# Four-layer attention and feed-forward kernel: a schedule table for the two threads of its middle layers

## The reference

```python
# layer 1, feed-forward: gated low-rank experts on a base product
base = jnp.einsum('bsd,od->bso', x, W_base) + b_base
gate = jax.nn.softmax(xf @ W_gate.T, axis=-1)
thr = jax.nn.sigmoid(xf @ W_thr + b_thr[0]) * MAX_THRESHOLD
adapted = gate - thr[:, None]
...
h = jnp.einsum('nd,erd->ner', xf, A_w)
moe = jnp.einsum('ner,ne,eor->no', h, w, B_w) * SCALING
# layer 2, attention: group-wise products with the context, a group norm over y
t = jnp.einsum('oc,bcd->bod', Wt, inp_v)
p = jnp.einsum('oc,bcd->bod', Wp, inp_q)
g = jnp.einsum('oc,bcd->bod', Wg, inp_k)
...
return yn * gn_w[None, :, None] + gn_b[None, :, None] + residual
# layer 2, feed-forward: 16 heads of 32 features on permuted columns
t = jnp.einsum('bhd,hdm->bhm', t, up)
t = jax.nn.gelu(t, approximate=False)
t = jnp.einsum('bhm,hmd->bhd', t, down)
```

## Time and profile before

| | us |
|---|---|
| median of 3 runs | 1979.35 |
| lowest and highest | 1978.04, 1983.15 |
| the profiled execution | 1980.43 |
| its span, from first to last instruction | 1978.6 |
| busy in the span: PE | 1773.6 |
| busy: DVE | 1457.3 |
| busy: POOL | 1094.7 |
| busy: ACT | 1066.9 |

### The profile page before, as it was taken

One profiled execution on the slowest core, in us unless ns is written; L12 is line 12 of the kernel. 1 busy time (PEld: TensorE's weight loads), 2 busy tenths in 40 slices (PEclk: granted clock), 3 DMA queues, 4 the chain that ended last, 5 costly groups with the idle time before them and its releaser, 6 DMA issues.

```text
span 1978.6 us, 26146 instructions
## 1 busy us (share of the span) xinstructions
PE 1773.6 (90%) x8645; PEld 1452.4 (73%) x8645; DVE 1457.3 (74%) x2518; ACT 1066.9 (54%) x2555; POOL 1094.7 (55%) x970
## 2 busy tenths in 40 slices
PE   6877899999999999887777699999999999879989
PEld 4655778878887888675455578888888888768777
DVE  6974798998999975676453588888888888848730
ACT  5335677777787775521334254655555545536520
POOL 7666575565565654533533366766767768526600
PEclk8878999999999999897776899999999999989999
DMA  3011211112111210200002111111111111011111
GB/s 128 1 59 40 57 57 48 49 49 69 55 43 49 70 49 23 80 25 0 0 0 80 43 38 34 38 53 38 38 38 54 33 38 38 24 49 61 44 52 38
DMA packets 54134, 88.06 MB, mean 45 GB/s; under 512 B 9008, under 2 KB 15792, under 8 KB 53744
## 3 DMA queue, kind: packets, MB, share of 16 engines
q1 hardware_dynamic: 54000, 86.39, 14.1%
HBM read 75.62 MB, written 10.75 MB: 44 GB/s over the span
## 4 chain that ended last, share of the span: by engine, by line
DVE 23%; PE 19%; issue 18%; POOLq 13%; POOL 12%; ACT 8%; DVEq 6%; DMA 0%; SPq 0%; ACTq 0%
POOLq L284 7%; DVE b_st_u L211 7%; PE e_ps L66 6%; POOLq L282 5%; DVEq L212 4%; PE c_ps L66 3%; POOL d_roped L1093 3%; PE b_ps_o L66 2%; PE b_ps_job L66 2%; POOL d_pt_sign L281 2%; ACT b_st_sign L192 2%; PE a_ps L66 2%; POOL d_wo L1098 1%; DVEq L136 1%; POOL d_wq L1098 1%
## 5 line engine op out<-in xcount | busy, mean ns | idle before, releaser
L66 PE MATMUL b_ps_o<-b_wo,b_oT 128*128 128x512 f32 x768 | 190.2, 397 | 20.4 <-DVE b_oT L1340 20.4
L66 PE MATMUL d_ps_o<-d_wo,d_oT 128*128 128x512 f32 x768 | 193.3, 401 | 12.2 <-DVE d_oT L1339 12.2
L281 POOL TENSOR_SCALAR b_pt_sign<-b_pt_sign 128x512 f32<-128x512 f32 x112 | 81.3, 726 | 206.9 <-ACT b_pt_sign L273 196.8
L66 PE MATMUL d_ps_job<-xnT,d_wq 128*128 128x512 f32 x768 | 193.3, 404 | 2.3 <-DVE d_rot_b L1349 2.3
L66 PE MATMUL b_ps_job<-xnT,b_wq 128*128 128x512 f32 x768 | 190.2, 401 | 4.8 <-DVE b_qT L1340 4.7
L66 PEld LDWEIGHTS b_ps_o<-b_wo,b_oT 128*128 128x128 f32 x768 | 145.4, 191 | 56.3 <-DVE b_oT L1340 26.2
L1093 POOL TENSOR_TENSOR d_roped<-d_rot_a,d_rot_b 128x512 f32<-128x512 f32 x80 | 104.7, 1309 | 144.1 <-DVE d_rot_b L1349 144.1
L211 DVE SCALAR_TENSOR_TENSOR b_st_u<-b_st_sign,b_st_u 128x512 f32<-128x512 bf16 x182 | 176.5, 970 | 9.5 <-issue 0.9
L66 PEld LDWEIGHTS d_ps_o<-d_wo,d_oT 128*128 128x128 f32 x768 | 144.8, 191 | 51.8 <-DVE d_oT L1339 18.9
L66 PEld LDWEIGHTS b_ps_job<-xnT,b_wq 128*128 128x128 f32 x768 | 143.1, 191 | 35.8 <-issue 6.7
L66 PEld LDWEIGHTS d_ps_job<-xnT,d_wq 128*128 128x128 f32 x768 | 143.1, 191 | 33.8 <-issue 3.5
(11 more groups left out here) (359 smaller groups left out, 4344.1 us busy)
## 6 DMA issues: line engine op xcount, KB each, us to landing
b_raw<-in_wq_dram SPq DMA_DIRECT2D x32, 256.0 KB, 2.6
b_raw<-in_wo_dram SPq DMA_DIRECT2D x32, 256.0 KB, 2.7
d_raw<-in_wq_dram SPq DMA_DIRECT2D x32, 256.0 KB, 2.6
d_raw<-in_wo_dram SPq DMA_DIRECT2D x32, 256.0 KB, 2.7
e_nat<-dequantized SPq DMA_DIRECT2D x30, 256.0 KB, 3.1
b_st_v<-in_quantized_dram SPq DMA_DIRECT2D x13, 256.0 KB, 2.9
dequantized<-b_st_u SPq DMA_DIRECT2D x13, 256.0 KB, 2.8
a_ctx_in<-in_ctx_dram SPq DMA_DIRECT2D x8, 256.0 KB, 5.3
```

Source lines behind the costliest of these rows:

```text
L66: i = pe.matmul(out, a, b, start=first and t == 0, stop=last and t == len(terms) - 1)
L281: pool.tensor_scalar(sign, sign, 0.5 * NF4_RISES[k], 0.0 if k else 0.5 * sum(NF4_RISES[:14]) - 1.0, ALU.mult, ALU.add)
```

## The change

It replaces stage c's `START` by a table in the form of stage a's: a due time for every step of each thread and engine. The steps are cut up so that each can be placed alone: the base products become steps of their own (`base`), ahead of or between those of the gates, with the four results of `low` packed in two banks to leave the others free. Norm statistics are taken tile by tile. In the up phase the gelu writes back into its PSUM bank, the high part is copied from the bank, and the low part is made by DVE instead of POOL, since it now reads PSUM; `up` h + 3 waits for that DVE step where it waited for the gelu. `tables` moves on DVE from 36 to 20.44, ahead of `z` of thread 0. SBUF is laid out anew so that stage d's first buffers are free earlier: its weight DMAs are due at D_AT - 119, its context DMAs at D_AT - 55.5, its splits' low parts go from DVE to POOL, and its first products are placed ahead of thread 1's `t4`. D_AT moves to C_AT + 224.5.

```diff
-        SPLITS = [("w", 0), ("ctx", 0), ("w", 1), ("w", 2), ("ctx", 1), ("ctx", 2), ("ctx", 3), ("w", 3), ("w", 4), ("w", 5)]
-        FIRST = [n for kind, n in SPLITS if kind == "w"]
+        FIRST = [n for kind, n, _ in SPLITS if kind == "w"]
 
         def split_at(kind, n):
-            return READ + PITCH * SPLITS.index((kind, n))
...
             def weights():
-                yield READ - 10.0
+                yield T + LOADS[0]
                 ready(sp, 0)
-                for kind, n in SPLITS[0:7]:
-                    if kind == "w":
-                        load(n)
-                    else:
-                        sp.dma_start(ctx_raw[:, n], ctxT_dram[:, n]).then_inc(s_ctx[n], 16)
+                for n in range(RAW):
+                    load(n)
                 for n in range(RAW, PER * n_groups):
                     yield low_at(n - RAW) + 0.05
                     load(n)
 
+            def contexts():
+                yield T + LOADS[1]
+                ready(sp, 1)
+                for n in range(K_CH):
+                    sp.dma_start(ctx_raw[:, n], ctxT_dram[:, n]).then_inc(s_ctx[n], 16)
+
...
-                ready(sp, 1)
+                yield T + LOADS[2]
+                ready(sp, 2)
...
-    LATER = 38.0
-    START = {"cs": (-18, 0.7), "g": (-13, 1.5), "rates": (-6, 0), "t1": (5, 2.2), "low": (13.5, 1.4), "gates": (20, 0), "hT": (30.5, 0),
-             "ffn": (33, 3.6), "norm2": (48, 0), "xs": (53, 1.3), "p": (57, 0.9), "grp": (61, 0), "y2": (64, 0.8), "x2": (64.2, 0.8),
-             "norm3": (68, 0), "t3": (73, 1.0), "pick": (77, 2.0), "up": (86, 1.5), "down": (96.5, 6.0), "out": (118, 2.0),
-             "norm4": (127, 0), "t4": (132, 1.0)}
-    PREPARED = {"wg": -18.5, "wm": -18, "wp": -17.5, "thr": -7, "wl": -4, "wb": 2, "wB": 14, "down": 28.5, "up": 35, "tables": 36}
     EARLY, RAW, OVER = -37.5, -14.5, 13.0
...
+    TIMES = {
...
+        ("pe", "low"): (13.5, 18.48, 21.12, 23.76, 40.61, 45.59, 49.73, 52.31),
...
+        ("pe", "t3"): (95.83, 96.66, 97.8, 98.8, 115.92, 117.49, 118.32, 120.14),
...
+        ("pe", "down"): (121.14, 133.8, 153.42, 164.52, 145.62, 161.22, 172.91, 188.22),
+        ("pe", "out"): (169.79, 176.21, 179.33, 182.45, 193.84, 196.72, 199.11, 201.5),
...
+        ("act", "gelu"): (110.83, 113.95, 115.41, 116.27, 118.14, 120.59, 127.73, 130.85, 139.63, 144.55, 145.93, 150.28, 152.26, 154.24, 158.77, 160.66,
...
+        ("act", "acts"): (111.69, 114.81, 117.54, 119.41, 124.61, 125.8, 128.59, 131.71, 141.01, 146.62, 147.39, 151.66, 156.89, 160.06, 161.35, 162.64,
...
+        ("dve", "z"): (26.07, 54.16),
...
+        ("dve", "thr"): (-7,), ("dve", "tables"): (20.44,)}
...
+        low_bank = lambda t: banks(t)[:, 0:2].rearrange("p b n -> p (b n)").rearrange("p (j n) -> p j n", n=LOW_PITCH)
+        base_bank = lambda t, j: bank(t, (2, 3, 1, 0)[j])
...
-                for h in H:
-                    yield at(t, "up", h + 1)
-                    waits(pool, t, ("act", "acts", h))
-                    done(pool.tensor_tensor(acts[t][:, 1, h % 4], act_f[t][:, h % 4], acts[t][:, 0, h % 4], ALU.subtract), ("acts", h))
...
+            def base(t):
+                for j in J:
+                    yield at("pe", "base", t, j)
+                    prepared(pe, "w_wb")
+                    waits(pe, t, ("dve", "t1", j), (("dve", "t1", 2), ("dve", "t1", 3), ("dve", "hw", 0), ("dve", "hT", 0))[j])
+                    product(pe, base_bank(t, j), [[xT(t, a, j)[:, c] for a in (0, 1)] for c in range(K_CH)],
                             [hi_lo(wb, c) for c in range(K_CH)], last=False)
...
                     c, r = divmod(h, 4)
                     rows = slice(32 * r, 32 * r + 32)
-                    waits(pe, t, ("dve", "pick", c if h >= 3 else h))
-                    if h >= 3:
-                        waits(pe, t, ("act", "gelu", h - 3))
-                    done(product(pe, bank(t, h % 3), [[up[rows, a, c] for a in (0, 1)]], [[xp[t][rows, a, c] for a in (0, 1)]]), ("up", h))
...
+                    yield at("pe", "up", t, h)
+                    prepared(pe, "w_up")
+                    waits(pe, t, ("dve", "pick", c), ("dve", "acts", h - 3) if h >= 3 else ("dve", "pick", h))
+                    pe_s[t].done(product(pe, bank(t, h % 3), [[up[rows, a, c] for a in (0, 1)]], [[xp[t][rows, a, c] for a in (0, 1)]]), ("up", h))
...
+            def gelus(t):
+                for h in H:
+                    yield at("act", "gelu", t, h)
                     waits(act, t, ("pe", "up", h))
-                    if h >= 4:
-                        waits(act, t, ("pool", "acts", h - 4))
-                    done(act.activation(act_f[t][:, h % 4], bank(t, h % 3), ACT.Gelu), ("gelu", h))
...
+            def highs(t):
+                for h in H:
...
                     if h >= 4:
                         waits(act, t, ("pe", "down", h // 4 - 1))
-                    done(act.copy(acts[t][:, 0, h % 4], act_f[t][:, h % 4]), ("acts", h))
...
+                    act_s[t].done(act.copy(acts[t][:, 0, h % 4], bank(t, h % 3)), ("acts", h))
...
+            def act_lows(t):
+                for h in H:
+                    yield at("dve", "acts", t, h)
+                    waits(dve, t, ("act", "acts", h))
+                    dve_s[t].done(dve.tensor_tensor(acts[t][:, 1, h % 4], bank(t, h % 3), acts[t][:, 0, h % 4], ALU.subtract), ("acts", h))
...
         def ready(eng, n):
 
 
-            waits(eng, 1, ("pe", "out" if n == 2 else "y2", 3))
-            waits(eng, int(n == 3), ("dve", "t4", 3))
+
+            if n == 0:
+                waits_all(eng, 1, ("pe", "y2"))
+                waits_all(eng, 0, ("dve", "p"), ("pool", "xc"))
+            if n == 1:
+                waits_all(eng, 0, ("pe", "down"))
+                waits_all(eng, 1, ("pool", "xb"))
+            if n in (2, 3):
+                waits_all(eng, 0, ("dve", "t4"))
+            if n == 3:
+                waits_all(eng, 1, ("pe", "out"))
+            if n == 4:
+                waits_all(eng, 1, ("dve", "t4"))
 
...
-    D_AT = C_AT + 193.0
+    D_AT = C_AT + 224.5
...
+    D_LOADS = (-119.0, -55.5, -25.0)
+    D_SPLITS = [("w", 0, -108.0), ("w", 1, -106.0), ("w", 2, -104.0), ("w", 3, -100.0), ("w", 4, -98.0),
+                ("ctx", 0, -42.0), ("ctx", 1, -39.0), ("ctx", 2, -36.0), ("ctx", 3, -33.0), ("w", 5, -24.5)]
...
-        d, d_over = grouped_attention(nc, stack, D_AT, D_AT - 50.0, 2.7, "vector", "d_", resid, xnT, w["ctxT"], w["gqa3"], w["tables3"], codes, None, (21, 8), c_ready, (-20.0, -18.0, -10.0, -5.0))
+        d, d_over = grouped_attention(nc, stack, D_AT, D_LOADS, D_SPLITS, "gpsimd", "d_", resid, xnT, w["ctxT"], w["gqa3"], w["tables3"], codes, None, (21, 8), c_ready, FIRST_UNITS)
```

621 lines of the change are left out of this document (318 added, 303 removed), and 46 rows, old and new, of the table TIMES.

## The result

The changed kernel takes 1917.91 us, the median of four runs (1915.94 to 1919.5), beside 1978.69 for the kernel before on the same chip: a ratio of 0.9692, with a 95% interval of 0.9669 to 0.9714. The profiled execution took 1918.22 us with a span of 1916.4, 62.2 less than before. In a later set of runs the same kernel took 1919.54 (ratio 0.9707, 0.9694 to 0.9721).

What follows compares the result with a forecast made beforehand. Stage c was taken as bound by waits in a circle, at a low clock. Stage c's 35.6 us and stage d's start's 6.2 us made 41.8 us: 1979.35 - 41.8 = 1937.6, say 1938 us, range 1920 to 1965.

Steps and rivals of the forecast that it cites:

- The factor: Stage c: trace time over table time, taken from stage a as 1.072, so 203.5 us for the table's 189.9.
- the factor is nearly 1 or below it: Rival, stage c: table steps may be longer than the engines'; at 1.00 time 1924, at 0.93 1911; chance 0.18.
- The clock: PE in stage c: with fewer gaps the granted clock was expected above 0.77; no size given.
- the low bound of 0.93 for the factor: Stage c: PE's estimated work of about 176 us, at a clock of 0.77, over the table's 189.9.
- `tables` costs nothing: DVE, stage c: moved ahead of `z`, the block takes 3.9 us after its DMAs land at 860.0, nothing beyond the factor.
- The bank and the gelu: Up phase: gelu in its bank taken as 0.607 us, DVE's subtraction as 0.691, bank held 1.9 us a turn.
- the other end: Up phase: gelu written to its bank takes 0.760 us by row L1832, adding 0.8 us a thread.
- the 20 that would have spoken against the forecast: Up phase: prediction wrong if PE's idle time put down to DVE's subtractions is more than some 20 us in sum.
- Stage d's start: From stage c's last `out` to stage d's first scores: 30.8 us against 37.0, 6.2 us saved.
- The splits on POOL: Stage d: splits take 2.6 us each on POOL; thread 0's root for `t4` could lose up to 2.6, taken as 0.
- threads hold each other up: Rival, stage c: in-order engines let a late step stop the other thread; factor 1.12 to 1.26, 1946 to 1973; chance 0.24.
- The signs: Profile after: `t3` of thread 1 some 110 us behind first `low`; wrong if first scores come after 1105 or before 1070.

Runs made afterwards that it cites:

- The three doubled steps: Changed kernel with one up-phase step made twice, a run each: subtraction on DVE 1931.17 us, copy on ACT 1930.67 us, `up` product on PE 1926.22 us.

## Why the prediction was wrong, point by point

**The factor is the step that failed.** I took the whole of stage a, 170.2 us for 158.8 in its table, as a rate of 1.072 and laid it on the 189.9 us of stage c: 203.5. Measured were 184.6, a factor of 0.972. That is 18.9 us, and the whole miss is 19.0. The factor was the wrong size, for two reasons. First, stage a's lag is no rate. PE in the kernel before, at the first product due at 47.2 (`we`) and the last `out` of stage a, due at 146.4:

```profile
52.10 2.93 PE L66 MATMUL a_ps<-a_wT,a_dft 128*128 128x512 f32 x6 [1.57 <-DVE a_wT L828]
...
152.58 1.63 PE L66 MATMUL a_ps<-a_wprod,a_dft 128*128 128x512 f32 x6 [1.04 <-POOL a_wprod L574]
```

4.9 of the 11.4 us are there by the first of them, 5.2 come in the last 22 us ahead of stage b, and between the two it is 100.5 us for 99.2, 1.013. These rows stood in the trace that I had. With 1.013, stage c would take 192.4 us, and the forecast would have been 1926, still 8 us too long.

Second, the rest, 7.8 us, is the up phase, 71.7 us for the 79.5 that 1.013 would give; the parts ahead of it and behind it are 1 us shorter and 1 us longer. In the changed kernel stage c runs at 96.5 us for the table's 96.3 up to the first `up` (1.003), at 71.7 for 78.5 in the up phase (0.914), and at 16.3 for 15.2 from the last `down` on. The table counts 0.86 from a gelu to its copy where the gelu takes 0.597 (L1937), and 3.3 from a `down` to the next step on PE, where six of the eight `down` take about 3.0 (the other two 4.48 and 4.58). My rival "the factor is nearly 1 or below it" said this, with the right row, and I gave it 0.18 because of stage a, "where the same held"; stage a has no such phase. The three doubled steps show that the length of a step counts there whichever engine does it, but what share of the 0.914 each too-long number has, no run tells.

**The clock.** I wrote that it would rise above 0.77 and gave that no term; even the floor of 176 us was PE's work at 0.77, so the low bound of 0.93 for the factor was no bound. (By the busy times above the work was 178.9 us, not 176.) Measured are 150.8 us of PE work at 0.91. A forecast that prices 26.4 us of idle time and lets the same 178.9 us of matmuls stand gets half of the gain. The factor of stage a had that stage's clock in it, 0.84 between 52 and 152 us, and I did not look at it.

**`tables` costs nothing: wrong.** The DMAs had landed, as forecast, but the block took 8.5 us and not 3.9, since POOL was at work. PE stood for 7.34 us, `z` of thread 0 came 18.7 us behind the first `low` and not 13.5, and moving the block gave 4.3 us back. I took the block's duration from a row of a time in which POOL was idle.

**The bank and the gelu: right.** The gelu in its bank takes 0.597 us (L1937, 32 times), where I took 0.607 and the other end was 0.760. The sentence of the Trainium skill that I set against that end (ScalarE: Activation LUTs, Step-by-step: what each stage is for), that writing PSUM is faster than writing SBUF, has the sign of 0.597 against 0.601 to 0.602 in the run with low parts on POOL; that is under 1% and no term of a sum. The subtraction takes 0.689 where I took 0.691, and PE waits 9.3 us for them, under the 20 that would have spoken against the forecast.

**Stage d's start: right.** 30.8 us forecast, 31.6 measured; the third q product at +18.9 forecast, 1052.54 - 1033.38 = 19.2 measured. Why it is shorter than before was half right: the run with the products behind `t4` still has 34.6, so 3.0 of the 5.4 us are the early products, and 2.4 come with the rest of the change.

**The splits on POOL: the price right, its place wrong.** They take 2.4 us each (2.6 forecast), and thread 0's root for `t4` starts 0.6 us late behind one of them, as feared. What I didn't see is DVE beside them, first POOL and then DVE in the changed kernel:

```profile
1017.88 4.88 POOL L1090 TENSOR_TENSOR d_ctxT<-d_ctx_raw,d_ctxT 128x1024 fp32r<-128x1024 f32 x2
```

```profile
1017.94 5.55 DVE L317 TENSOR_SCALAR c_xn<-resid,c_norm_mean_var,c_norm_rstd 128x512 f32<-128x512 f32 x3 [1.14 <-POOL c_norm_rstd L314]
...
1024.61 0.53 DVE L317 TENSOR_SCALAR c_xn<-resid,c_norm_mean_var,c_norm_rstd 128x512 f32<-128x512 f32 x1
```

Three steps of the norm took 5.55 us where the fourth, alone, took 0.53. PE's waits for `xn4` of thread 0 there are 1.82 and 0.67 us.

**The rival "threads hold each other up"**, 0.24, was the wrong place for the chance: with thread 1 at a constant distance stage c runs at 223.3 for 208.9, a factor of 1.069, and with the threads mixed it is 0.972. So the mixing did not make the kernel fall behind its table. (The table of the shifted run was only moved, not made for that distance.)

**The signs.** `t3` of thread 1 comes 101.9 us behind the first `low` (950.57 - 848.69), where some 110 were forecast. The first scores come at 1064.86, before the 1070 that I had named as a sign of being wrong; that is the factor again, since from the last `out` to the scores it took the time that was forecast.

## What to carry to other kernels

A lag between a table of due times and a trace is not a rate until it is read at three or four points; take it apart into the start, the middle and the end, and compare each kind of step's number in the table with its row. Where PE waits in gaps, read the time in two terms, the idle time and the busy time of the same matmuls at the granted clock: here the two gave about the same (26.4 and 28.1 us). Don't take the second for a fixed multiple of the first: the experiments contradict that. And take the duration of a DVE step from a row in which POOL does what it will do at the new place.
